# Folding and key stage: VectorE copies the turned context, and each group's high and low parts are made one slot later

## Chip, cores and metric

One core of a Trainium2 chip runs the whole program. The metric is its device time in microseconds; the median of three runs of the kernel before is 4688.49 us (4686.85 to 4693.32).

## What is computed

A decoder layer on 4 x 1024 tokens of width 512: windowed attention, cross attention with a context of 4 x 2048 x 384, state-space convolution and MLPs. The stage of this study prepares operands for later stages. Reduced to that:

```
K = x_vision @ Wk                       # keys: [8192, 384] @ [384, 128]
V = x_vision @ Wv                       # c_t = attn_mean @ V
film = c_t @ W_film_in, c_t @ W_film_out # so Wv @ W_film is made once (12 pieces)
h = einsum('bsd,dh->bsh', x, W_exp) + b_exp
h = butterfly(h, up_weights)            # 11 stages; the linear maps are folded into
h = gelu(h + up_bias)                   # W_exp (w3, b3) and W_con (w4) beforehand
h = butterfly(h, down_weights)
y = einsum('bsh,hd->bsd', h, W_con) + b_con
```

Keys are kept as a high part (the product rounded to fp32r) and a low part (the product less its high part).

## The kernel before

`decoder_layer` runs eight stages one after the other; each ends with all engines meeting. The second, `stage_butterfly_keys`, runs from about 270 to 569 us and merges three jobs on the same engines: folding the butterfly into the MLP weights, the film products, and the keys.

*Keys.* The context is cut in KG = 16 groups of 512 rows. For each group g SyncE loads `raw[g % 2]` (`context`, L603), TensorE turns its three 128-column parts in PE `keys_step` (L695, twelve transposes) into the two banks of `ps_t`, three copies (L840, on ScalarE) bring them to `cT` (which lies in the storage of `wx`, so the trace says `bf_wx`), and `project` (L681) multiplies them with `wk` into `ps_k`, which is the second bank of `ps_t`. TensorE runs `project(g - 1)` behind the turning of g. ScalarE writes the high part (`keys_hi`, L832), VectorE the low part (`keys_lo`, L939), SyncE stores both (`keys_stored`, L607). The second third of a turning waits until the low part of two groups before has been read out of the shared bank.

*Folding.* 4 top butterfly stages run over the down weights and later over the up weights (`group(1, i, g)`, i and g from 0 to 3). For each of 8 pairs ScalarE makes two scaled halves (`partners`, L812, L813), and VectorE makes a group of two pairs of them (L922, L927; four instructions). With i = 1 and 2 ScalarE also copies the turned down blocks (`down_copied`, L820) and the down products (`product_copied`, L826).

*Film.* Twelve products (`film`, L729), two banks; VectorE copies each (`film_copied`, L935) and SyncE stores it.

The order on each engine is written out by hand as interleaved loops; engines meet by semaphores only. TensorE: groups 0 and 1 with film 0 and 1; then groups 2 to 5 each with one film product; then the 16 down products (L766), with a key group behind every second one (groups 6 to 12) and film 6 and 7 in the middle; then groups 13 to 15 with film 8 to 10, the last `project`, film 11; last the row turning (L789), whose results are stored as w3. SyncE's queue has the stores of film 0 to 5 ahead of those of w4, and a load of context between w4's. ScalarE's `keys_step(g)` copies group g, then makes the high part of g - 1; VectorE's `keys_lo` follows behind a folding group and ahead of the film copy.

## Time and profile before

| | before |
|---|---|
| median of 3 runs, us | 4688.49 (4686.85 to 4693.32) |
| profiled execution, us | 4691.36, its span 4689.3 |
| mean granted TensorE clock | 0.927 |
| TensorE busy over the span | 3982.0 us (85%) |
| VectorE | 2527.2 us (54%) |
| ScalarE | 1470.2 us (31%) |
| GpSimd | 2009.3 us (43%) |

The profile is one execution. Its views used here: the stretches (busy time of each engine between two times), the waits (which instruction waited for which), the timeline of an engine (start, duration and idle time before each instruction, neighbours merged), and the groups of instructions by line. A granted clock of 1.0 is 2.4 GHz, 0.5 is 1.2 GHz.

### The profile page before, as it was taken

The page shows a single profiled execution, that of the slowest core. Times are in us where ns is not written, and L with a number is a line of the kernel's source. Part 1 is how long each engine was busy: PE and PEld are TensorE (multiplying, and loading weights), DVE is VectorE, ACT ScalarE, POOL GpSimd, SP SyncE. Part 2 cuts the span into 40 slices and gives each one's busy share as a digit, 9 for nine tenths or more (in the row PEclk, how much of TensorE's full clock was granted, in tenths as well). Part 3 has the DMA queues.
Part 4 walks back from the last instruction along what each step waited for, and adds up shares of the span by engine and source line. Part 5 has one row for each costly group of instructions (what it writes and reads, how often), then busy time and mean ns, then how long its engine had stood idle before and what let it go on. Part 6 is the DMA issues. An engine that isn't in the chain of part 4 may idle for free. (4 is left out here: it accounts for less than half of the span.)

```text
span 4689.3 us, 63710 instructions
## 1 busy us (share of the span) xinstructions
PE 3982.0 (85%) x20972; PEld 3269.0 (70%) x20972; DVE 2527.2 (54%) x8700; ACT 1470.2 (31%) x2339; POOL 2009.3 (43%) x1399
## 2 busy tenths in 40 slices
PE   6747599986866888888699697968999999999998
PEld 3633277765766778777688575757778877878886
DVE  8733355548888888888355555224344336222222
ACT  2344333325645666666200101212111112111111
POOL 0000011115756777777566042014677665333332
PEclk8659899997988999999799898988999999999999
DMA  1154522222010010100243333342222123000000
GB/s 59 37 167 153 169 77 90 83 70 59 15 45 28 25 52 15 49 28 12 83 147 134 109 118 134 115 131 88 64 70 77 60 76 97 25 21 25 22 25 18
DMA packets 248656, 336.41 MB, mean 72 GB/s; under 512 B 67587, under 2 KB 125859, under 8 KB 246053
## 3 DMA queue, kind: packets, MB, share of 16 engines
q1 hardware_dynamic: 156420, 186.18, 13.0%
q10 hardware_dynamic: 89392, 138.45, 8.7%
q0 software_dynamic: 2560, 8.39, 0.5%
q8 instruction: 130, 2.13, 0.2%
q14 instruction: 154, 1.25, 0.1%
HBM read 220.70 MB, written 112.25 MB: 71 GB/s over the span
## 5 line engine op out<-in xcount | busy, mean ns | idle before, releaser
L1647 PE MATMUL xa_ps_t<-xa_diag,xa_s_buf 128*128 128x128 f32 x4096 | 524.8, 289 | 139.7 <-ACT xa_a L1734 74.8
L2808 POOL TENSOR_TENSOR m_act_hl<-m_g,m_act_hl 128x512 fp32r<-128x512 f32 x256 | 355.6, 1389 | 660.0 <-DVE m_act_hl L3114 660.0
L1647 PEld LDWEIGHTS xa_ps_t<-xa_diag,xa_s_buf 128*128 128x128 f32 x4096 | 512.7, 204 | 160.5 <-issue 80.5
L3114 DVE CAST m_act_hl<-m_g 128x512 fp32r<-128x512 f32 x256 | 137.8, 538 | 832.2 <-ACT m_g L2982 832.2
L1811 DVE MAX8 xa_cand<-xa_s_buf 128x8 f32<-128x64 f32 x4096 | 543.0, 219 | 65.6 <-ACT xa_s_buf L1697 40.4
L2982 ACT ACTIVATE m_g<-m_ps_h,m_b 128x512 f32<-128x512 f32 x256 | 176.2, 688 | 1096.5 <-PE m_ps_h L82 1091.5
L80 PE MATMUL m_ps_h<-m_hT,m_w 128*128 128x512 f32 x1024 | 414.1, 404 | 6.3 <-issue 4.3
L80 PE MATMUL m_ps_o<-m_w,m_act_hl 128*128 128x512 f32 x1024 | 406.8, 397 | 0.7 <-POOL m_act_hl L2808 0.7
L82 PE MATMUL m_ps_h<-m_hT,m_w 128*128 128x512 f32 x1024 | 406.7, 397 | 0.0
L81 PE MATMUL m_ps_h<-m_hT,m_w 128*128 128x512 f32 x1024 | 406.7, 397 | 0.0
L82 PE MATMUL m_ps_o<-m_w,m_act_hl 128*128 128x512 f32 x1024 | 406.6, 397 | 0.0
L81 PE MATMUL m_ps_o<-m_w,m_act_hl 128*128 128x512 f32 x1024 | 406.4, 397 | 0.0
L1575 POOL TENSOR_SCALAR xa_s_buf<-xa_s_buf,xa_top 128x1024 f32<-128x1024 f32 x120 | 342.3, 2853 | 141.8 <-ACT xa_prob L1716 141.8
L1577 POOL TENSOR_TENSOR xa_s_buf<-xa_s_buf,xa_prob 128x1024 f32<-128x1024 f32 x120 | 321.1, 2676 | 18.2 <-issue 0.9
L1697 ACT ACTIVATE xa_s_buf<-xa_ps_s 128x2048 f32<-128x2048 f32 x128 | 239.6, 1872 | 145.3 <-PE xa_ps_t L1647 79.1
L1716 ACT ACTIVATE xa_prob<-xa_s_buf,xa_nmax 128x2048 f32<-128x2048 f32 x128 | 252.6, 1998 | 89.9 <-POOL xa_s_buf L1577 89.9
L1614 PE MATMUL xa_ps_s<-xa_ks,xa_qs 128*128 128x512 f32 x512 | 159.3, 435 | 126.8 <-ACT xa_s_buf L1697 111.7
L80 PEld LDWEIGHTS m_ps_h<-m_hT,m_w 128*128 128x128 f32 x1024 | 193.6, 189 | 56.1 <-issue 11.3
L80 PEld LDWEIGHTS m_ps_o<-m_w,m_act_hl 128*128 128x128 f32 x1024 | 193.2, 189 | 48.8 <-POOL m_act_hl L2808 1.9
L82 PEld LDWEIGHTS m_ps_h<-m_hT,m_w 128*128 128x128 f32 x1024 | 193.8, 189 | 47.1
L82 PEld LDWEIGHTS m_ps_o<-m_w,m_act_hl 128*128 128x128 f32 x1024 | 193.6, 189 | 47.0
L81 PEld LDWEIGHTS m_ps_o<-m_w,m_act_hl 128*128 128x128 f32 x1024 | 193.3, 189 | 47.0
(373 smaller groups left out, 8370.4 us busy)
## 6 DMA issues: line engine op xcount, KB each, us to landing
at_xk<-in_x_dram SPq DMA_DIRECT2D x128, 128.0 KB, 2.7
spectrum<-df_yo ACTq DMA_DIRECT2D x32, 512.0 KB, 2.8
id_raw<-spectrum SPq DMA_DIRECT2D x32, 512.0 KB, 5.7
m_xt<-x ACTq DMA_DIRECT2D x64, 256.0 KB, 3.8
bf_raw<-in_ctx_dram SPq DMA_DIRECT2D x16, 768.0 KB, 4.7
xa_ks<-kt SPq DMA_DIRECT2D x48, 256.0 KB
xa_raw<-in_ctx_dram SPq DMA_DIRECT2D x32, 384.0 KB, 3.4
kt<-bf_khl SPq DMA_DIRECT2D x16, 512.0 KB, 2.8
```

The source lines that it names most:

```text
L80: pe.matmul(out, w_hi, m_lo, start=start, stop=False)
L81: pe.matmul(out, w_lo, m_hi, start=False, stop=False)
L82: return pe.matmul(out, w_hi, m_hi, start=False, stop=stop)
L1575: pool.tensor_scalar(half, half, top[:, t % 2, h, TOPK - 1:TOPK], None, ALU.is_ge)
L1577: pool.tensor_tensor(half, half, prob[:, h % 2, HALF:S2], ALU.mult).then_inc(s_psel, 1)
L1614: last = pe.matmul(ps_s[:, c, :], qs[:, t % 2, h, :], ks[:, h, c * 512:(c + 1) * 512], start=True, stop=True)
L1647: last = pe.matmul(ps_t[:, c // 4, c % 4, :], s_buf[:, t % 2, h, k0:k0 + P], diag[:, h, :], start=(h == 0 and c % 4 == 0), stop=(h == HEAD ...
L1697: act.activation(s_buf[:, t % 2, h, :], ps_s[:, :, :].rearrange("p c n -> p (c n)"), ACT.Copy).then_inc(s_sc, 1)
L1716: act.activation(prob[:, h % 2, :], s_buf[:, t % 2, h, :], ACT.Exp, bias=nmax[:, t % 2, h:h + 1], scale=SCALE).then_inc(s_exp, 1)
L1811: dve.max(out=ranks[h][:, :, g], in_=s_buf[:, t % 2, h, :].rearrange("p (n g e) -> p g n e", g=SEGS, e=4)[:, g, :, :])
L2808: pool.tensor_tensor(lo, g32[:, :], hi.bitcast(F32), ALU.subtract).then_inc(s_gl, 1)
L2982: act.activation(g32[:, :], ps_h[:, n % 2, :], ACT.Gelu, bias=b1[:, cur, n:n + 1]).then_inc(s_g, 1)
```

## The change

VectorE gets a `keys_step(g)`: low part of g - 2, a wait for the key product of g - 2, then the three copies of the turned group g into `cT`. ScalarE loses its `keys_step` with the 48 copies and keeps `keys_hi`, called for one group earlier at each place (a slot later for a given group). On SyncE the store of a key group is also a step later (g - 2 instead of g - 1), and the last one stands behind all film stores. TensorE's order and all waits of TensorE are the same.

```diff
--- before.py
+++ after.py
@@ -610,8 +610,8 @@
                 def keys_step(g):
                     if g + 2 < KG:
                         context(g + 2)
-                    if g >= 1:
-                        keys_stored(g - 1)
+                    if g >= 2:
+                        keys_stored(g - 2)
 
                 sp.wait_ge(s_wx[1], 16)
                 sp.dma_start(wv[:, :, :], A["L0_xattn_Wv"].rearrange("(c p) n -> p c n", p=P)).then_inc(s_wv, 16)
@@ -645,9 +645,10 @@
                 for n in range(FILM, FILM + 3):
                     keys_step(KG - 3 + n - FILM)
                     film_stored(n)
-                keys_stored(KG - 1)
+                keys_stored(KG - 2)
                 for n in range(FILM + 3, 2 * FILM):
                     film_stored(n)
+                keys_stored(KG - 1)
                 for n in range(4 * DC):
                     sp.wait_ge(s_rc[n % 2], n // 2 + 1)
                     c, g = n // 4, n % 4
@@ -831,16 +832,6 @@
                         act.wait_ge(s_kst[g % 2], 16 * (g // 2))
                     act.activation(khl[:, g % 2, 0, :], ps_k[:, :], ACT.Copy).then_inc(s_khi, 1)
 
-                def keys_step(g):
-                    if g >= 2:
-                        act.wait_ge(s_k, g - 1)
-                    for c in range(VC):
-                        n = VC * g + c
-                        act.wait_ge(s_t, n + 1)
-                        act.activation(cT[:, g % 2, c, :], ps_t[:, c % 2, :], ACT.Copy).then_inc(s_tc, 1)
-                    if g >= 1:
-                        keys_hi(g - 1)
-
                 act.wait_ge(s_cdn, 16 * 4)
                 for q in range(HC // 2):
                     if q % 2 == 0:
@@ -866,13 +857,11 @@
                         h = (HC // 2) * (i - 2) + q
                         act.wait_ge(s_mm, h + 1)
                         act.activation(wT[:, h, 0:D], ps[:, h % 2, :], ACT.Copy).then_inc(s_mmc, 1)
-                keys_step(0)
-                keys_step(1)
                 for i in range(TOP):
                     for q in range(HC // 2):
                         partners(1, i, q)
                         if i == 0 and q % 2 == 1:
-                            keys_step(2 + q // 2)
+                            keys_hi(q // 2)
                         if i == 1:
                             if q == 0:
                                 down_copied(0)
@@ -883,9 +872,10 @@
                             if h + 2 < HC:
                                 down_copied(h + 2)
                             if h % 2 == 1 and h < HC - 1:
-                                keys_step(FILM + h // 2)
+                                keys_hi(FILM - 2 + h // 2)
                         if i == TOP - 1 and q in (1, 3, 5):
-                            keys_step(KG - 3 + q // 2)
+                            keys_hi(KG - 5 + q // 2)
+                keys_hi(KG - 2)
                 keys_hi(KG - 1)
                 for n in range(0, 16, 2):
                     act.wait_ge(s_r, n + 1)
@@ -937,6 +927,14 @@
                 def keys_lo(g):
                     dve.wait_ge(s_khi, g + 1)
                     dve.tensor_tensor(khl[:, g % 2, 1, :], ps_k[:, :], khl[:, g % 2, 0, :].bitcast(F32), ALU.subtract).then_inc(s_klo, 1)
+
+                def keys_step(g):
+                    if g >= 2:
+                        keys_lo(g - 2)
+                        dve.wait_ge(s_k, g - 1)
+                    for c in range(VC):
+                        dve.wait_ge(s_t, VC * g + c + 1)
+                        dve.tensor_copy(cT[:, g % 2, c, :], ps_t[:, c % 2, :]).then_inc(s_tc, 1)
 
                 dve.wait_ge(s_cdn, 16 * 4)
                 for g in range(GROUPS):
@@ -962,16 +960,17 @@
                 dve.drain().then_inc(s_bias, 1)
                 dve.wait_ge(s_ms, 16)
                 dve.tensor_scalar(mask[:, :], mask_u8[:, :], BIG, -BIG, ALU.mult, ALU.add).then_inc(s_mask, 1)
-                keys_lo(0)
+                keys_step(0)
+                keys_step(1)
                 for i in range(TOP):
                     for g in range(GROUPS):
                         group(1, i, g)
                         if i < 2:
-                            keys_lo(GROUPS * i + g + 1)
-                        elif i == 3:
-                            keys_lo(KG - GROUPS + g)
+                            keys_step(GROUPS * i + g + 2)
                         elif g < GROUPS - 1:
-                            keys_lo(2 * GROUPS + g + 1)
+                            keys_step(GROUPS * i + g + 2 - (i - 2))
+                        elif i == TOP - 1:
+                            keys_lo(KG - 2)
                         if i == 0:
                             film_copied(g)
                         if i == 1 and GROUPS + g < FILM:
@@ -980,6 +979,7 @@
                             film_copied(FILM + g)
                 for n in range(FILM + GROUPS, 2 * FILM):
                     film_copied(n)
+                keys_lo(KG - 1)
                 dve.tensor_tensor(upb[:, :], upb[:, :], wT[:, :, D], ALU.add)
                 dve.drain().then_inc(s_hi, 1)
                 for n in range(1, 16, 2):
```

## Rows read from the trace of the kernel before

**Rows 1.** stretches: busy us of each engine (instructions), TensorE's granted clock, DMA share, GB/s

```profile
357.00:538.00 181.00, 135.35 (x431) 67.09 (x430) 73.81 (x111) 88.44 (x165) 0.00 (x0) 0.94 0.45 157
```

**Rows 2.** waits from 357 to 538 us: us in total, times, longest

```profile
PE bf_ps_w L729 <- DVE bf_fo L935: 16.6, 8, 2.1
```

**Rows 3.** timeline of TensorE, one film slot: start us, us, line, idle before and releaser

```profile
402.61 1.04 PE L695 MATMUL bf_ps_t<-bf_ident,bf_raw 128*128 128x128 f32 x8
...
404.45 2.84 PE L681 MATMUL bf_ps_t<-bf_wx,bf_wk 128*128 128x512 f32 x6
409.36 3.70 PE L729 MATMUL bf_ps_w<-bf_low_up,bf_wvT 128*128 128x512 f32 x8 [2.07 <-DVE bf_fo L935]
412.89 1.04 PE L695 MATMUL bf_ps_t<-bf_ident,bf_raw 128*128 128x128 f32 x8
```

**Rows 4.** timelines of ScalarE and VectorE, the same slot

```profile
403.31 1.08 ACT L840 ACTIVATE bf_wx<-bf_ps_t 128x512 f32<-128x512 f32 x2 [3.23 <-PE bf_ps_t L695]
...
407.32 0.60 ACT L832 ACTIVATE bf_khl<-bf_ps_t 128x512 fp32r<-128x512 f32 x1 [2.08 <-PE bf_ps_t L681]
...
407.95 0.69 DVE L939 TENSOR_TENSOR bf_khl<-bf_ps_t,bf_khl 128x512 fp32r<-128x512 f32 x1 [4.92 <-ACT bf_khl L832]
408.56 0.74 DVE L935 TENSOR_SCALAR bf_fo<-bf_ps_w,bf_gate 128x512 f32<-128x512 f32 x1
410.40 1.42 DVE L922 SCALAR_TENSOR_TENSOR bf_wT<-bf_wT,bf_col_up,bf_part 128x513 f32<-128x513 f32 x2 [1.10 <-ACT bf_part L813]
411.90 1.42 DVE L927 SCALAR_TENSOR_TENSOR bf_wT<-bf_wT,bf_col_up,bf_part 128x513 f32<-128x513 f32 x2
```

**Rows 5.** groups of instructions by line, 200 to 1100 us: busy us, mean ns, idle before

```profile
L840 ACT ACTIVATE bf_wx<-bf_ps_t 128x512 f32<-128x512 f32 x48 | 27.3, 603 | 36.2 <-PE bf_ps_t L695 36.2
...
L988 DVE COPY bf_out_t<-bf_ps 128x512 f32<-128x512 f32 x8 | 5.5, 692 | 16.3 <-DMA w<-bf_out_t 13.8 <-PE bf_ps L789 2.5
```

**Rows 6.** timelines of VectorE and TensorE at the start of the keys

```profile
368.72 0.67 DVE L939 TENSOR_TENSOR bf_khl<-bf_ps_t,bf_khl 128x512 fp32r<-128x512 f32 x1
...
378.18 2.98 PE L695 MATMUL bf_ps_t<-bf_ident,bf_raw 128*128 128x128 f32 x12 [5.28 <-DMA bf_raw<-in_ctx_dram]
380.95 4.12 PE L681 MATMUL bf_ps_t<-bf_wx,bf_wk 128*128 128x512 f32 x6
```

**Rows 7.** timeline of TensorE in the down product and the tail

```profile
428.65 2.84 PE L681 MATMUL bf_ps_t<-bf_wx,bf_wk 128*128 128x512 f32 x6
431.33 0.27 PE L756 MATMUL bf_ps_e<-bf_ident,bf_e_dn 128*128 128x128 f32 x1
...
451.82 2.82 PE L681 MATMUL bf_ps_t<-bf_wx,bf_wk 128*128 128x512 f32 x6
...
465.13 2.84 PE L681 MATMUL bf_ps_t<-bf_wx,bf_wk 128*128 128x512 f32 x6
...
489.89 2.84 PE L681 MATMUL bf_ps_t<-bf_wx,bf_wk 128*128 128x512 f32 x6
...
500.66 3.97 PE L681 MATMUL bf_ps_t<-bf_wx,bf_wk 128*128 128x512 f32 x6
...
539.16 1.04 PE L789 MATMUL bf_ps<-bf_ident,bf_wT 128*128 128x128 f32 x8
```

**Rows 8.** timelines of ScalarE and VectorE in the down product

```profile
444.75 0.60 ACT L826 ACTIVATE bf_out_t<-bf_ps 128x512 f32<-128x512 f32 x1 [3.15 <-DMA w<-bf_out_t]
...
478.45 0.28 ACT L820 ACTIVATE bf_eT<-bf_ps_e 128x128 f32<-128x128 f32 x1
478.61 0.73 ACT L812 ACTIVATE bf_part<-bf_wT,bf_col_up 128x513 f32<-128x513 f32 x1
...
479.98 1.42 DVE L922 SCALAR_TENSOR_TENSOR bf_wT<-bf_wT,bf_col_up,bf_part 128x513 f32<-128x513 f32 x2 [2.40 <-ACT bf_part L813]
```

**Rows 9.** timeline of TensorE in a later stage: a wait of 2.97 us

```profile
1456.99 6.33 PE L1647 MATMUL xa_ps_t<-xa_diag,xa_s_buf 128*128 128x128 f32 x32 [2.97 <-ACT xa_a L1734]
```

**Rows 10.** stretch right behind that wait, columns as in the first group

```profile
1457.00:1461.00 4.00, 4.00 (x19) 4.00 (x20) 3.71 (x26) 0.74 (x2) 4.00 (x3) 0.50 0.42 129
```

## The prediction

> **What bounds the kernel now.** The page's span is the whole program; the edit touches one stage only, which runs from about 270 to 569 us, and in it the stretch from 357 us, where the first context group is turned, to 539 us, where the row turning (L789) begins. So I read, in this order: the busy times of that stretch, its waits, then the timelines of TensorE, ScalarE and VectorE side by side, slot by slot. Over 181 us TensorE is busy 135 us, ScalarE 88 and VectorE 74 [rows 1]: no engine is full, so waits between engines set the pace, and TensorE, in whose order everything hangs, is nearest to the bound. Its costliest wait on VectorE is the film product for the film copy (L729 on L935), 16.6 us in 8 waits [rows 2]; the timeline of a film slot shows where it comes from. The turning starts at 402.61, the key product (L681) at 404.45, the film product only at 409.36, the next turning at 412.89 [rows 3]: a slot of 10.28 us. The key product needs 2.68 us (428.65 to 431.33, [rows 7]), so 4.91 - 2.68 = 2.2 us of each slot are a wait: VectorE's film copy (408.56) stands behind the low part (407.95), which stands behind ScalarE's high part (407.32), which waits for this slot's key product [rows 4].
>
> In the second part (down product, 423 to 500 us) a steady slot takes (489.89 - 465.13)/3 = 8.25 us between key products [rows 7]. There ScalarE is the chain: high part, partners, product copy, block copy, partners, product copy, block copy, three context copies. All other stages only move with the end of this one, so the sum is made here.
>
> **Part 1: film slots, T(3) to the end of film(5).** (T(g) is the turning of context group g, P(g) the start of its key product; P(g-1) runs in the slot of T(g).) The high part a slot later takes the 2.2 us wait away: the film copy no longer stands behind this slot's key product. What it costs: a VectorE copy from PSUM takes 692 ns against ScalarE's 603 [rows 5], and neighbours start 0.61 apart (407.95, 408.56) against 0.48 (the pair at 403.31 takes 1.08) [rows 4]. From turning to key product it was 1.84 us [rows 3]; with the first copy's start 0.70 after the turning, + 0.61 + 0.69 + 0.05, it becomes 2.05. New slot: 2.05 + 2.68 + 3.53 (film, 409.36 to 412.89) = 8.26 us. Is VectorE fast enough? From its first copy x: third copy x + 1.43, film copy x + 2.04, folding group x + 2.7 for 3.0 us (two halves 1.50 apart, [rows 4]), low part x + 5.7 to 6.4. The bank is wanted at about x + 7.6 + 0.4: it is in time by 1.6 us. ScalarE has only 2.5 us of partners and 0.6 of high part per slot. Three slots give 3 x 2.02 = **-6.0 us**.
>
> **Part 2: the start.** ScalarE copied groups 0 and 1 at 359 to 364 us, while VectorE made the down blocks; VectorE now comes to them only where low part 0 began, 368.72 [rows 6]. TensorE stands with the last third of T(0) from 358.3 to 369.4 and then runs at the lower clock. Copies 0.69, T(0)'s last third 1.1, copy, T(1) 2.0, copy: P(0) at about 374.1, 4.1 us at the low clock (the row at 380.95 has 4.12, against 2.84 [rows 6, 7]), film(0) and film(1) 7 us: T(2) at 385 instead of 378.18. The old T(2) waited for a load and paid the low clock itself: 378.18 to T(3) at 392.3, 14.1 us. The new one, warm, takes 8.3: T(3) at 393.3, **+1.0 us** (-1.3 with a warm first product, +3 with one film product at the low clock). The load of group 2 isn't late: it is issued at 370.7 and had 10 us before.
>
> **Part 3: entry to the down product.** Here ScalarE's order bites. Its partners for the second of a group's two pairs stand behind a block copy (down_copied), which needs a block turned on TensorE *after* the key product; VectorE now does that folding group before the low part and the copies, and so before the next key product can start. Before, ScalarE copied the context while VectorE folded beside it. First slot, on the old clock of rows: group from 427.0 (unchanged) to 430.0, low part 0.6, copies: P(5) at 432.1 instead of 428.65 [rows 7]: **+3.5 us**.
>
> **Part 4: the steady loop.** From P: key product 2.68, block turned 0.27 + 0.04 (the row at 431.33), block copy, partners 0.16 later, group 1.53 after the block copy (478.45 to 479.98) [rows 8], so the group starts at P + 4.5; folding 3.0; low part at P + 7.5; then 0.61 + 0.72 (turning into the freed bank) + 0.1 + 0.69 to the next P: P + 9.63. As a check the old chain added in the same way gives 8.26 and the rows 8.25. Three steady slots P(8) to P(11): 3 x 1.38 = **+4.1 us**. P(11) to P(12) took 10.77 (489.89 to 500.66 [rows 7]) since two pairs and product copies lie between; the new chain (product copy of block 15 at P + 3.7, four partners to 6.8, group to 9.8, 2.1) is 12.2 with a cold start: **+1.4 us**.
>
> **Part 5: P(5) to P(8),** before 428.65 to 465.13, 36.5 us, with a stall that stays: SyncE keeps the first stores of w4 and the load of group 8 behind film_stored(5), so ScalarE waits to 444.75 [rows 8]. The film copy 5 comes at about 442.3 (old clock; before 441.0), ScalarE then starts at 446.0, group to 451, P(7) at 453.4 against 451.82 [rows 7]; then two film products, as before, and P(8) at 467.1. 432.1 to 467.1 is 35.0: **-1.5 us**. The store of key part g now is issued one step later; the high part of g + 2 needs it, and has more than 4 us over in every slot, at the stall about none.
>
> **Part 6: the tail, P(12) to the row turning,** before 500.66 to 539.16, 38.5 us, with four waits for the film copy. New: key product at the low clock 3.9, film 3.5, turning 2.05 (P(13) at 9.5), slot 8.3, then 6.2 and 6.2: 30.2. **-8.3 us**. **Part 7: the end.** The last low part (0.6) now comes behind the last film copy and its 512 KB store into the stores of w3, which fill the DMA engines: **+1.0 us** (0.6 to 1.6).
>
> Sum: -6.0 + 1.0 + 3.5 + 4.1 + 1.4 - 1.5 - 8.3 + 1.0 = -4.8 us.
>
> **The clock.** The new loop leaves TensorE idle about 3.1 us in one piece per slot (from the first third of the turning at P + 5.1 to P + 8.25), before at most 1.5. The trace has no such gap in this stage; the nearest: 2.2 us gaps left 1.0 in nearly all film slots (one beside the low clock of 387), while a gap of 2.97 us at 1456.99 is followed by 0.50 [rows 9, 10], which is the 1.2 GHz level. A key product at it costs 4.12 - 2.84 = 1.3 us. Bounds: none of the loop's slots, 0, to all six (P(5), P(6), P(9) to P(12)) at 1.9 with the turning, 11. I take three slots at 1.2, **+3.5**, nearer the row of 2.97 than that of 2.2 but mostly with part of the product. The Trainium skill (TensorE: Matmul & The Clock Gate, "HAM oscillation") says that a loop with such a wait pays the transition in every iteration; by it the sum would be near the upper bound. The rows here bear it out for 2.97 us and not for 2.2.
>
> Net -1.3 us on the profiled execution's own 4691.36 (span 4689.3 and 2.1 around it), which lies 2.9 above the median of the three runs shown; on the median 4688.49: **4687.2 us**. About 0.2% (9.4 us) is what a measurement of this kernel can tell from no change.
>
> **The rivals.** *Gaps throttle TensorE (slower):* all six gaps bring the low clock (+11), and at the start a film product too (+2): -4.8 + 13 = +8, with the end at its upper bound and another cold slot at the stall +10: 4698 us. It turns slower once the clock falls in more than three loop slots. For: the row at 1456.99 [rows 9, 10]; against: the key product is only partly in the slow time where it falls. 0.20 in all, of it 0.11 over 0.2%. *The loop does not close (faster):* if ScalarE's partners were ready early, a slot of the down product would be 7.2 us (key product, two down products, high and low part, copy): Part 3 falls to 0, Part 4 to -3.2 and -1: -4.8 - 3.5 - 7.3 - 2.4 = -18, 4670 us. For: ScalarE loses 29 us of copies; against: the written order puts down_copied ahead of the second partners, and nothing in the change moves it. 0.07. *The film gains stay and the clock holds (mildly faster):* -4.8 to -11 us, 4679, when the start costs nothing either: 0.20, of it 0.07 beyond 0.2%. *Nothing arrives at the end,* as the final stores of w3 and the wait for them fill what was gained: 4688, 0.10. The forecast, gains and losses cancelling within some 5 us: 0.43.
>
> **The numbers.** Leaving out half of the two far cases, the range runs from 4677 to 4698. Faster by over 0.2%: 0.07 + 0.07 = 0.14; slower by over 0.2%: 0.11; within: 0.75.
>
> **What would show it.** T(2) at about 385 us; no wait of L729 on the film copy; film slots 8.3 us and the film stretch over near 418 instead of 423; from there slots of about 9.6 us with the folding group, low part and three copies in a row on VectorE, and ScalarE's second partners waiting on a block turned after the key product; the row turning near 534 to 538 instead of 539.2. Wrong if the slots there are nearer 7 (the loop does not close) or 11 (clock), if VectorE's low part is late in the film slots, or if a load of context shows up ahead of a turning.

## The result, and the profile after

| | before | after |
|---|---|---|
| time, median of 11 runs each, us | 4688.49 (4682.72 to 4694.88) | 4698.27 (4694.53 to 4706.42) |
| ratio after / before, 95% interval | | 1.0021 (1.0013 to 1.0029) |
| profiled execution, us (span) | 4691.36 (4689.3) | 4704.4 (4702.4) |
| first context turning T(0) / row turning / first instruction of the attention stage, us | 357.25 / 539.16 / 569.9 | 356.42 / 543.40 / 576.9 |

The change costs 9.8 us, 0.21%. The forecast was 4687.2 us, -1.3, with a range that ended at 4698: the time lies just above its end, and the sign is that of the rival "gaps throttle TensorE". The two profiled executions differ by 13 us, and 7 of these have arisen when the attention stage begins. All medians in this document leave out two executions that took far longer than the rest, one of before (6561.55 us) and one of e9_bias_hidden (8547.19 us).

First the same stretch as [rows 1] in the profile after (busy us of TensorE, its weight loads, VectorE, ScalarE, GpSimd, each with its instructions, then TensorE's granted clock, DMA share, GB/s), with a window over the steady loop:

```profile
357.00:538.00 181.00, 138.43 (x417) 70.68 (x415) 103.05 (x157) 60.53 (x114) 0.00 (x0) 0.86 0.46 151
...
465.00:490.00 25.00, 18.37 (x61) 9.78 (x60) 13.40 (x20) 10.31 (x21) 0.00 (x0) 0.84 0.46 147
```

As the edit says, 28 to 29 us of work have gone from ScalarE to VectorE. TensorE has done less of its work in the stretch (417 instructions for 431) in more busy time: the granted clock fell from 0.94 to 0.86. The waits of the same stretch (us in total, times, longest):

```profile
DVE bf_wT L912 <- ACT bf_part L814: 42.2, 8, 8.5
...
PE bf_ps_t L696 <- DVE bf_khl L929: 25.1, 8, 6.5
...
PE bf_ps_t L696 <- DVE bf_wx L937: 14.5, 8, 11.1
...
ACT bf_out_t L827 <- DMA w<-bf_out_t: 7.4, 1, 7.4
...
ACT bf_khl L833 <- DMA kt<-bf_khl: 3.6, 1, 3.6
```

The wait of the film product for the film copy [rows 2] is in the whole list no more. In its place TensorE waits at the turning (L696) for VectorE's low part (L929), which stands behind the folding group (L912), which waits for ScalarE's partners. The 11.1 us is the start; the last line was not in the forecast.

TensorE in a film slot of after (start us, us, line, idle before and releaser), the slot that answers to [rows 3]:

```profile
400.50 1.04 PE L696 MATMUL bf_ps_t<-bf_ident,bf_raw 128*128 128x128 f32 x8
401.95 0.66 PE L696 MATMUL bf_ps_t<-bf_ident,bf_raw 128*128 128x128 f32 x4 [0.42 <-DVE bf_wx L937]
402.55 2.84 PE L682 MATMUL bf_ps_t<-bf_wx,bf_wk 128*128 128x512 f32 x6
405.23 3.60 PE L730 MATMUL bf_ps_w<-bf_low_up,bf_wvT 128*128 128x512 f32 x8
408.66 0.60 PE L696 MATMUL bf_ps_t<-bf_ident,bf_raw 128*128 128x128 f32 x4
```

The film product follows the key product at once, and the slot takes 8.16 us instead of 10.28. Now TensorE in the down product, where [rows 7] had 8.25 us from key product to key product (L682):

```profile
467.13 2.84 PE L682 MATMUL bf_ps_t<-bf_wx,bf_wk 128*128 128x512 f32 x6 [0.19 <-DVE bf_wx L937]
469.92 1.02 PE L767 MATMUL bf_ps<-bf_wc,bf_eT 128*128 128x512 f32 x2
470.89 1.02 PE L767 MATMUL bf_ps<-bf_wc,bf_eT 128*128 128x512 f32 x2
471.75 0.60 PE L696 MATMUL bf_ps_t<-bf_ident,bf_raw 128*128 128x128 f32 x4
475.43 1.97 PE L696 MATMUL bf_ps_t<-bf_ident,bf_raw 128*128 128x128 f32 x8 [3.08 <-DVE bf_khl L929]
477.33 5.04 PE L682 MATMUL bf_ps_t<-bf_wx,bf_wk 128*128 128x512 f32 x6
482.32 1.02 PE L767 MATMUL bf_ps<-bf_wc,bf_eT 128*128 128x512 f32 x2
483.29 1.02 PE L767 MATMUL bf_ps<-bf_wc,bf_eT 128*128 128x512 f32 x2
484.15 0.60 PE L696 MATMUL bf_ps_t<-bf_ident,bf_raw 128*128 128x128 f32 x4
487.83 1.57 PE L696 MATMUL bf_ps_t<-bf_ident,bf_raw 128*128 128x128 f32 x8 [3.08 <-DVE bf_khl L929]
489.28 4.20 PE L682 MATMUL bf_ps_t<-bf_wx,bf_wk 128*128 128x512 f32 x6
```

Each slot has the wait of 3.08 us that the forecast worked out (3.1), and behind it a key product of 5.04 or 4.20 us where 2.84 is the time at full clock; two turned thirds take 1.97 and 1.57 instead of 1.25. The slots are 10.2 and 12.0 us. VectorE in the same slot is the loop in one view:

```profile
471.65 1.42 DVE L912 SCALAR_TENSOR_TENSOR bf_wT<-bf_wT,bf_col_up,bf_part 128x513 f32<-128x513 f32 x2 [3.98 <-ACT bf_part L814]
473.15 1.42 DVE L917 SCALAR_TENSOR_TENSOR bf_wT<-bf_wT,bf_col_up,bf_part 128x513 f32<-128x513 f32 x2
474.69 0.69 DVE L929 TENSOR_TENSOR bf_khl<-bf_ps_t,bf_khl 128x512 fp32r<-128x512 f32 x1
475.29 0.68 DVE L937 COPY bf_wx<-bf_ps_t 128x512 f32<-128x512 f32 x1
476.59 0.69 DVE L937 COPY bf_wx<-bf_ps_t 128x512 f32<-128x512 f32 x1 [0.61 <-PE bf_ps_t L696]
477.44 0.69 DVE L937 COPY bf_wx<-bf_ps_t 128x512 f32<-128x512 f32 x1 [0.16 <-PE bf_ps_t L696]
```

The key product of 467.13 is over at 469.92, then block, partners, a folding group of 3.0 us, low part, copies, next key product. The group is the longest link, and nothing in the low part or the copies needs it: it only stands ahead in VectorE's order. And ScalarE waits in its turn for the block turned behind the slow key product:

```profile
482.52 0.28 ACT L821 ACTIVATE bf_eT<-bf_ps_e 128x128 f32<-128x128 f32 x1 [8.06 <-PE bf_ps_e L757]
```

### The profile page after: what moved, and what is told of

It reads as the page before. It is cut to its first block and busy times, and to the rows that moved or that the text cites. A ratio compares the mean times of both kernels' runs of the same rounds, so it can differ in the third digit from the quotient of the medians.

```text
span 4702.4 us, 63710 instructions
## 1 busy us (share of the span) xinstructions
PE 3992.6 (85%) x20972; PEld 3276.8 (70%) x20972; DVE 2560.9 (54%) x8748; ACT 1443.6 (31%) x2291; POOL 2008.4 (43%) x1399
## 5 line engine op out<-in xcount | busy, mean ns | idle before, releaser
L1564 POOL TENSOR_TENSOR xa_aT<-xa_a,xa_aT 128x512 fp32r<-128x512 f32 x128 | 161.9, 1284 | 153.5 <-ACT xa_a L1734 153.5
L80 PEld LDWEIGHTS m_ps_o<-m_w,m_act_hl 128*128 128x128 f32 x1024 | 193.2, 189 | 48.8 <-POOL m_act_hl L2808 2.0
L82 PEld LDWEIGHTS m_ps_o<-m_w,m_act_hl 128*128 128x128 f32 x1024 | 193.6, 189 | 47.0
```

The costliest lines, as they stand in the source:

```text
L80: pe.matmul(out, w_hi, m_lo, start=start, stop=False)
L82: return pe.matmul(out, w_hi, m_hi, start=False, stop=stop)
L1564: pool.tensor_tensor(aT[:, 1, 4 * g:4 * g + 4, :], a32[:, g % 2, :, :], aT[:, 0, 4 * g:4 * g + 4, :].bitcast(F32), ALU.subtract).then_inc( ...
```

## The experiments

Counted from T(0), the traces give these times (us; P(g) is the start of group g's key product, as in the forecast; the last column is how long the attention stage takes). The time of a run is compared with runs of the kernel before on the same chip. Two of the kernels are before and after once more.

```
kernel             P(5)   P(8)-P(11)  P(12)  row turning  stage ends at  attention
before             71.4   24.8        143.4  181.9        569.9          489.9
before again       69.6   24.8        142.3  184.6        571.3          488.2
after              69.9   33.7        157.6  187.0        576.9          493.2
after again        70.2   31.9        157.0  187.0        574.4          492.2
e1_steps_first     66.7   23.5        141.8  171.4        560.3          490.2
e2_fill_gap        68.8   29.2        150.0  178.5        568.0          493.0
e3_scalar_start    63.8   32.8        151.1  180.8        568.6          494.2
e4_delay_alone     63.3   31.8        147.7  178.5        568.6          487.3
e5_copies_alone    79.4   36.4        171.5  214.8        601.9          491.1
e6_reordered       61.6   23.5        123.4  153.5        543.5          493.8
e7_bias_early      69.8   32.7        156.8  186.5        577.1          493.6
e8_before_padded   68.7   24.7        141.0  183.1        569.5          494.0
e9_bias_hidden     62.6   23.5        124.8  155.2        542.3          491.9
e10_padded_back    61.5   23.6        125.4  156.1        542.0          487.1
```

My theory after the result: the loop through the folding group (longer than before by 1.4 us a slot) and the low clock behind its waits cost what the film slots gain; rivals were the clock alone, the start, and the moved copies as such.

**The order on VectorE** (e1_steps_first). Edit on the kernel after: in the second film turn and the down product the folding group comes behind the low part and the copies.

```diff
                     for g in range(GROUPS):
-                        group(1, i, g)
+                        if i not in (1, 2):
+                            group(1, i, g)
...
                             keys_lo(KG - 2)
+                        if i in (1, 2):
+                            group(1, i, g)
```

> The changed kernel, but in the down product (i = 1 and 2) VectorE does the low part and the three context copies ahead of the folding group instead of behind it. Theory (order: the group, fed by ScalarE partners that wait for a block turned after the key product, stands in series with the next key product): P(8) to P(11) falls from 33.7 us to about 23 (7.7 a slot), TensorE's waits on the low part fall from 3.1 us to under 1, its clock stays at 1.0, P(5) starts 3 us after the last down product; the row turning starts 15 to 20 us earlier and the time is 4675 to 4682 us. Rival (VectorE's copies are simply dearer and slower than ScalarE's): the same copies at the same price, so the slots stay above the old 8.25 us and the time stays within 3 us of 4698.

Measured: 4684.08 us (4679.72 to 4691.04), before 4686.41; ratio 0.9995 (0.9986 to 1.0004). TensorE in the steady loop of this kernel:

```profile
469.61 2.84 PE L682 MATMUL bf_ps_t<-bf_wx,bf_wk 128*128 128x512 f32 x6 [0.19 <-DVE bf_wx L937]
...
476.02 1.25 PE L696 MATMUL bf_ps_t<-bf_ident,bf_raw 128*128 128x128 f32 x8 [1.19 <-DVE bf_khl L929]
477.45 2.84 PE L682 MATMUL bf_ps_t<-bf_wx,bf_wk 128*128 128x512 f32 x6 [0.18 <-DVE bf_wx L937]
```

The slot is 7.85 us, the wait 1.19, every key product of the loop is at full clock, and the row turning comes 15.6 us earlier than in after. So the folding group in VectorE's order is the loop's cause. The time itself, 14.2 us below after, ends up only level with before: 2 us above the expectation, where the stage ends 9.6 us earlier than before's. The attention stage, behind it, gives back none of this; what is lost there was found below.

**The clock by itself** (e2_fill_gap). Edit: the same waits stay, but TensorE turns identity tiles into the bank that isn't in use while it waits.

```diff
                             pe.wait_ge(s_tc, VC * g)
+                        if c == 0 and 6 <= g <= 13:
+                            for _ in range(16 if g < 13 else 40):
+                                pe.transpose(ps_t[:, 0, 0:P], ident[:, :], ident[:, :])
                         if c == 1 and g >= 2:
```

> The changed kernel with added work only: ahead of the first third of each turning of groups 6 to 12 TensorE turns the identity 16 times more, 40 times for group 13, into a bank that the real turning overwrites, so that its wait for the low part is partly filled (16 cost 1.8 us at the full clock). Theory, part two (the waits let the clock fall to 1.2 GHz): key products P(5) to P(12) return from 3.4-4.9 us to 2.7, which is 9.7 us in all, P(8) to P(11) falls from 33.7 to about 29 us, the time to about 4689. Rival (the order alone costs it, the clock matters little): the slots keep their 11.2 us and the time is 4698 or more.

Measured: 4693.13 us (4683.41 to 4695.66); ratio 1.0010 (1.0001 to 1.0019). In the window from 465 to 500 us TensorE's granted clock, 0.84 in after's loop, is here 1.00 (columns as above):

```profile
465.00:500.00 35.00, 30.45 (x157) 19.38 (x156) 18.96 (x28) 17.28 (x35) 0.00 (x0) 1.00 0.65 208
```

All key products of P(5) to P(12) take 2.81 to 2.84 us, P(8) to P(11) takes 29.2 us, three slots of 9.73, and the row turning comes 8.5 us earlier than in after. The time is 5.1 us below after, some 4 above the 4689 expected. The 16 identity turns also cost something where TensorE hardly had to wait: before the turning ahead of P(8) the wait was 0.28 us in after, and here VectorE's copies wait 1.62 us for TensorE at that place. So 8.5 us is less than the clock took. This splits the loop: 29.2 against before's 24.8 is the chain (+4.4; the forecast had +4.1), 33.7 against 29.2 is the clock (+4.5 for three slots, where the forecast had +3.5 for all).

**The start** (e3_scalar_start). Edit: ScalarE copies groups 0 and 1 again, VectorE's first two steps are gone.

```diff
+                for n in range(2 * VC):
+                    g, c = n // VC, n % VC
+                    act.wait_ge(s_t, n + 1)
+                    act.activation(cT[:, g % 2, c, :], ps_t[:, c % 2, :], ACT.Copy).then_inc(s_tc, 1)
                 for i in range(TOP):
                     for q in range(HC // 2):
...
-                keys_step(0)
-                keys_step(1)
```

> The changed kernel, but ScalarE copies groups 0 and 1 as before, VectorE the other fourteen. Theory: the start costs the change 1 us in net, since the old one waited for a load; T(2) comes at about 378 after the load instead of 384, at the low clock, and all of it shifts by 2 to 4 us: 4694 to 4697. Rival (the 11 us of idle TensorE at the start is the loss): T(2) 6 us earlier and the time 4692 or less.

Measured: 4690.10 us (4683.41 to 4698.64); ratio 1.0004 (0.9994 to 1.0013). The row turning comes 6.2 us earlier than in after, more than the 2 to 4 expected, and the time lies where the rival had it (4692 or less): T(2), in this kernel's TensorE timeline, waits for its load as in before [rows 6]

```profile
360.82 2.84 PE L682 MATMUL bf_ps_t<-bf_wx,bf_wk 128*128 128x512 f32 x6
363.50 7.03 PE L730 MATMUL bf_ps_w<-bf_low_up,bf_wvT 128*128 128x512 f32 x16
375.66 3.08 PE L696 MATMUL bf_ps_t<-bf_ident,bf_raw 128*128 128x128 f32 x12 [5.13 <-DMA bf_raw<-in_ctx_dram]
```

Counted from T(0), T(2) comes at 20.8 us (375.66 less 354.87), as in before (20.9), where after had 27.8 (384.17 less 356.42), and the film product behind it doesn't wait. So the start costs 6 us against what the late high part could have, though only 0.8 against before (T(3) at 392.33 less 356.42, before 392.3 less 357.25), whose own film product there had the wait for the film copy.

**The delay alone, on the kernel before** (e4_delay_alone). ScalarE keeps the copies, but makes a group's high part one slot later, VectorE the low part, SyncE the store.

```diff
                     if g >= 2:
                         act.wait_ge(s_k, g - 1)
+                        keys_hi(g - 2)
                     for c in range(VC):
...
-                    if g >= 1:
-                        keys_hi(g - 1)
...
                         if i < 2:
-                            keys_lo(GROUPS * i + g + 1)
+                            keys_lo(GROUPS * i + g)
                         elif i == 3:
-                            keys_lo(KG - GROUPS + g)
+                            keys_lo(KG - GROUPS + g - 1)
```

> The kernel before with the delay alone: high and low part of group g - 2 in the slot of group g, but ScalarE keeps all 48 copies. Theory (the low part behind the folding group is what ties the loop, not who copies): film slots lose their 2.2 us wait (8.1 us a slot), the slots of the down product go to 9.5 us and more with waits for the low part of about 3 us and the low clock, time within 5 us of the changed kernel, 4693 to 4700. Rival (moving the copies to VectorE makes the loop): the down slots stay at 8.25 and the film gain of some 14 us shows: 4676.

Measured: 4686.41 us (4679.57 to 4689.47); ratio 0.9996 (0.9987 to 1.0005). TensorE in its loop:

```profile
477.96 1.97 PE L696 MATMUL bf_ps_t<-bf_ident,bf_raw 128*128 128x128 f32 x8 [3.08 <-DVE bf_khl L940]
479.76 3.55 PE L682 MATMUL bf_ps_t<-bf_wx,bf_wk 128*128 128x512 f32 x6
```

The same wait of 3.08 us and the same low clock, with the copies still on ScalarE: P(8) to P(11) takes 31.8 us. The bad loop comes with the delay, since the low part sits behind this slot's folding group; the film slots are 8.2 us, so the gain comes with the delay too. But the time is that of before, not the 4693 to 4700 expected: the stage ends 8.3 us earlier than in after, of which the start is some 6, and the attention stage takes 487.3 us instead of 493.2, for a reason found below.

**The copies alone, no delay** (e5_copies_alone). On the kernel after, high part, low part and store go back to their old slot (ten lines; the core of them):

```diff
-                        keys_lo(g - 2)
                         dve.wait_ge(s_k, g - 1)
                     for c in range(VC):
                         dve.wait_ge(s_t, VC * g + c + 1)
                         dve.tensor_copy(cT[:, g % 2, c, :], ps_t[:, c % 2, :]).then_inc(s_tc, 1)
+                    if g >= 1:
+                        keys_lo(g - 1)
```

> The changed kernel without the delay: VectorE copies the context, but high and low part of group g - 1 stay in the slot of group g, as before the change. Theory (each of the two parts alone ties the down product's loop, since either the low part or the copies stand behind the folding group; the film gain is the delay's; the late start is the copies'): film slots 10.5 us with their wait for the film copy, T(2) at 384, P(8) to P(11) 28 to 33 us, the slowest kernel of all, 4702 to 4712 us. Rival (the two parts only do harm together): the down slots stay near 8.3 us and the time is 4690 to 4696.

Measured: 4723.02 us (4721.71 to 4724.16); ratio 1.0079 (1.0066 to 1.0093), slower than the 4702 to 4712 expected. Its waits from 357 to 570 us:

```profile
DVE bf_khl L928 <- ACT bf_khl L832: 51.3, 16, 4.7
...
PE bf_ps_w L729 <- DVE bf_fo L924: 16.6, 8, 2.1
```

Film slots are 10.5 to 12.2 us, the film product waits as before, and now VectorE itself stands 51.3 us at the low part, with the folding groups behind it. So the two halves of the change belong together: the copies on VectorE cost 30 to 33 us at the row turning without the delay, and with it 8.5 (after against the delay alone), of which 6 are the start.

**Putting the order right** (e6_reordered). On the kernel after: the two edits above (ScalarE's start, the group behind the step), the same order for the first group of the last turn with the high part of group 11 right behind the last product copy, the stores of film 4 and 5 moved on SyncE from ahead of the stores of w4 to between them, and the store of the 8 KB bias issued behind the first output copy (the edit of e7_bias_early below).

```diff
-                for n in range(FILM):
-                    if n < GROUPS:
-                        keys_step(2 + n)
+                for n in range(GROUPS):
+                    keys_step(2 + n)
                     film_stored(n)
...
+                    if n in (1, 3):
+                        film_stored(GROUPS + n // 2)
...
-                        group(1, i, g)
+                        late = i in (1, 2) or (i == TOP - 1 and g == 0)
+                        if not late:
+                            group(1, i, g)
...
+                        if i == TOP - 1 and g == 0:
+                            film_copied(FILM)
+                        if late:
+                            group(1, i, g)
...
-                            if h % 2 == 1 and h < HC - 1:
+                            if h % 2 == 1:
                                 keys_hi(FILM - 2 + h // 2)
```

> A version that may beat both, from the changed kernel: ScalarE copies groups 0 and 1; VectorE's low part and copies ahead of the folding group in the down product and for group 13, whose high part of group 11 comes right behind the last product copy; SyncE stores film 4 and 5 between the stores of w4 instead of ahead of them; the bias b3 is stored behind ScalarE's first row copy instead of its last. Theory: T(3) 5 us earlier, no wait of ScalarE for a store of w4 (4 us and the low clock behind it), no 6.4 us wait at group 13, no bias store at the end (some 5 us): the stage 18 to 28 us shorter than in the kernel before and 4660 to 4672 us. Rival (the stores of the stage fill the DMA engines, so that what is gained ahead is waited for at the end): no better than 4680.

Measured: 4666.52 us (4665.29 to 4670.39), before 4685.84; ratio 0.9961 (0.9947 to 0.9975), faster by 0.39%. The stage ends 26.4 us earlier than in before, but the time is only 19.3 lower. Again some us are lost behind the stage. Against e1_steps_first the row turning comes 17.9 us earlier: 5.1 of it are there at P(5) (the start), 9.5 arise from P(5) to P(8) (29.6 us for 39.1) and 3.8 from P(11) to P(12). In e1 ScalarE waited 8.2 us for a store of w4 and 3.4 us for the store of key part 4 between P(5) and P(8); here it waits for neither. So the largest part is put down to the two film stores, by the timelines: no kernel moved them alone.

**The end of the stage** (e7_bias_early). Edit on the kernel after: the bias store is issued after the first of the output copies, not after the last.

```diff
                     act.activation(out_t[:, n % 4, :], ps[:, n % 2, :], ACT.Copy).then_inc(s_rc[0], 1)
-                act.wait_ge(s_hi, 1)
-                act.dma_start(b3_out.rearrange("(c p) -> p c", p=P), upb[:, :], allow_slow_non_contiguous=True).then_inc(s_b3, 16)
+                    if n == 0:
+                        act.wait_ge(s_hi, 1)
+                        act.dma_start(b3_out.rearrange("(c p) -> p c", p=P), upb[:, :], allow_slow_non_contiguous=True).then_inc(s_b3, 16)
```

> The changed kernel with the bias store b3 issued behind ScalarE's first row copy instead of its last, nothing else. Theory (from the row turning's start the stage took 30.8 us before and 33.5 after; the last to land is this store, 12.8 us behind ScalarE's last copy): the turning to the next stage's start falls by 4 to 8 us and the time to 4691 to 4695. Rival (the last stores of w3 land as late, so the bias store is beside them): 33 us stay and the time stays at 4698.

Measured: 4701.45 us (4700.39 to 4703.63); ratio 1.0035 (1.0021 to 1.0049): no gain, the rival was right. The window behind the row turning in this kernel, where the bias store is in it:

```profile
545.00:560.00 15.00, 2.67 (x16) 1.99 (x16) 1.05 (x2) 1.19 (x2) 0.00 (x0) 0.66 1.08 114
```

and in after, where only the 256 KB stores are in it, then the window of the bias store there, with its size (KB) and its time to landing (us):

```profile
545.00:560.00 15.00, 9.40 (x56) 6.73 (x53) 5.58 (x9) 4.18 (x7) 0.00 (x0) 0.89 0.88 297
...
557.00:577.00 20.00, 0.98 (x7) 0.50 (x5) 1.37 (x2) 0.60 (x1) 0.07 (x1) 0.58 0.69 62
...
b<-bf_upb ACTq DMA_DIRECT2D x1, 8.0 KB, 12.8
```

By the edit's access pattern the 8 KB go out as 4-byte elements; in after they take 12.8 us to land. Placed among the 256 KB stores they leave the DMA engines as busy (share 1.08 for 0.88) but moving 114 GB/s instead of 297, and a row copy of ScalarE waits 12.8 us for a store of w3.

**Both kernels once more** (a2_after_again, b2_before_again), to see what belongs to the kernel and what to one execution.

> The changed kernel itself, once more: a second profile and its time on this chip. Theory: the same slots (P(8) to P(11) 32 to 35 us, since where the low clock begins shifts between executions), stage length within 3 us of the first, ratio 1.0015 to 1.003; the 6 us by which the stages behind this one were longer in the first profile (4125.5 against 4119.4 us) are of that execution alone, so here 4116 to 4128. Rival (VectorE's longer instruction stream costs something in the stages behind): again 4125 or more.

Measured: 4697.30 us (4693.0 to 4700.8); ratio 1.0025 (1.0014 to 1.0035). The row turning is at the same place to 0.1 us. The stages behind took 4121.3 us: within the 4116 to 4128 of the expectation, and not the 4125 of the rival; over all kernels (below) a part of the rival holds.

> The kernel before itself, once more, for a second profile: no VectorE wait of over 1 us without releaser in the attention stage, key products P(8) to P(11) 24.8 us apart at the full clock, turning start about 181.9 us behind T(0), the stages behind the folding stage within 3 us of 4119.

Measured: 4683.4 us in one execution. Row turning at 184.6 after T(0) instead of 181.9, stage end at 571.3, and the stages behind took 4110.1 us, not within 3 of 4119. So one execution of before can be 2.7 us later there, and the change's price at the row turning is 2.4 to 5.1 us.

**What is lost behind the stage.** Nothing that the change touches lies in the attention stage, yet it took 489.9 us in before and 493.2 in after. VectorE's and TensorE's timelines of after near 835 us show the place:

```profile
834.84 1.13 DVE L1339 TENSOR_SCALAR at_tT<-at_ps_t,at_u_k 128x128 f32<-128x128 f32 x4 [1.69 <-issue]
836.21 0.69 DVE L1328 SCALAR_TENSOR_TENSOR at_dot<-at_xq,at_u_q 128x512 f32<-128x512 f32 x1 [0.24 <-issue]
837.68 0.08 DVE L1328 DVE_READ_ACCUMULATOR at_dot<-at_xq,at_u_q 128x1 f32 x1 [0.78 <-issue]
```

```profile
836.05 3.10 PE L1184 MATMUL at_ps_s<-at_xT,at_tT 128*128 128x256 f32 x8 [2.12 <-DVEq L1340]
```

and the DMA queues of the window from 832 to 839 us have packets of instructions:

```profile
q14 instruction: 3, 0.02, 1.0%
```

VectorE's wait of 1.69 us has no releaser in the profile, and it is the only one of its kind over 1 us in the stage. The packets do not say which engine they feed, and alone they prove nothing: before has 16 packets of this queue in the stage and no such wait. TensorE waits 2.12 us for it, and its next product takes 3.10 us where the same 8 take 1.99 in the last kernel below. VectorE's trace has 11629 instructions in before and 11691 in after: 48 copies came in, and with their waits it is 62. My theory: the boundary between two pieces of VectorE's instruction stream has moved from somewhere harmless into the busy part of a block, with no link to what the change computes. The Trainium skill (Advanced Engine Details and Errata, "ISA Cache") has an engine's instruction cache in lines of 256 instructions; that section names no price.

Test (e8_before_padded): the kernel before with 62 one-column memsets on VectorE at the end of the stage, where it is idle, and nothing else.

```diff
+                for k in range(62):
+                    dve.memset(pad[:, k:k + 1], 0.0)
         st.clear()
```

> The kernel before with 62 small memsets added to VectorE behind its last row copy, where it is idle until the stage ends; the changed kernel's VectorE stream is 62 instructions longer too. Theory (in all kernels with the longer stream VectorE once waits for instructions in the attention stage, some 260 us into it, 1.7 and 0.8 us without any releaser, with three packets of an instruction queue beside it and the lower TensorE clock behind it, which costs 3 to 4 us; it belongs to where the stream is cut, not to the new order): the same stall at the same tile, folding stage as before, time 3 to 5 us above the kernel before. Rival (it comes from the new order or from ScalarE's shorter stream): no stall, time within 1 us of it.

Measured: 4692.44 us (4687.46 to 4699.53), before 4687.6; ratio 1.0012 (1.0003 to 1.0021). The same stall at the same tile, in VectorE's timeline:

```profile
828.23 1.13 DVE L1342 TENSOR_SCALAR at_tT<-at_ps_t,at_u_k 128x128 f32<-128x128 f32 x4 [1.66 <-issue]
...
831.39 0.08 DVE L1331 DVE_READ_ACCUMULATOR at_dot<-at_xq,at_u_q 128x1 f32 x1 [1.11 <-issue]
```

The attention stage takes 494.0 us. Instructions that do nothing, at an idle place, cost the kernel before 0.12%. So the wait belongs to the length of VectorE's instruction stream, whatever the added instructions do.

**The two remedies.** First on the reordered kernel (e9_bias_hidden): the bias is added right behind the last folding group instead of behind the last film copies, and its store goes out ahead of the last high part.

```diff
                 keys_hi(KG - 2)
+                act.wait_ge(s_hi, 1)
+                act.dma_start(b3_out.rearrange("(c p) -> p c", p=P), upb[:, :], allow_slow_non_contiguous=True).then_inc(s_b3, 16)
                 keys_hi(KG - 1)
...
                         elif i == TOP - 1:
+                            dve.tensor_tensor(upb[:, :], upb[:, :], wT[:, :, D], ALU.add)
+                            dve.drain().then_inc(s_hi, 1)
                             keys_lo(KG - 2)
```

> The reordered version (e6) with the bias computed right behind the last folding group and stored behind ScalarE's high part 14, ahead of the tail's film copies, instead of behind the first row copy. Theory (the bias store holds the DMA engines for 11 to 14 us wherever it stands, so it helps only where nothing else wants them): the row turning to the next stage's start falls from 33.7 us to about 26, the time to 4658 to 4662. Rival (then the stores of film 9 to 11 and of the last key parts wait for it and film copy 11 with them): the turning starts 4 to 6 us later and the time stays at 4666.

Measured: 4664.06 us (4661.61 to 4668.13), before 4687.6; ratio 0.9951 (0.9937 to 0.9964); 4658 to 4662 were expected. From the row turning to the stage's end it takes 30.2 us, for 33.7 in e6_reordered (543.5 - 356.3 - 153.5); 26 were expected. But the row turning itself comes 1.7 us later (155.2 for 153.5), so the stage ends only some 1.8 us earlier. Second, on that (e10_padded_back), 200 memsets on VectorE, so that its stream is 256 instructions longer than in before (56 from the copies, 200 of padding; pieces of 256, if there are such, would begin where they began):

```diff
+                for k in range(110):
+                    dve.memset(pad[:, k:k + 1], 0.0)
                 dve.wait_ge(s_cdn, 16 * 4)
...
+                for k in range(110, 200):
+                    dve.memset(pad[:, k:k + 1], 0.0)
```

> The version with the bias moved (e9), whose VectorE stream is 56 instructions longer than before's up to the attention stage, padded with 200 small memsets in VectorE's idle times of the folding stage, so that all behind lies 256 instructions later than in the kernel before. Theory (VectorE's stream is loaded in pieces of a fixed number of instructions, 256 or a divisor of it, and the stall belongs to a boundary): no 1.7 us wait without releaser in the attention stage, which takes 488 to 490 us instead of 491.9, and 4660 to 4663 us. Rival (what counts is the total length or the shorter ScalarE stream, or the pieces have another size): the stall stays or moves, time 4665 or more.

Measured: 4656.12 us (4651.18 to 4659.95), before 4689.41; ratio 0.9925 (0.9912 to 0.9939), the fastest kernel here, 0.75% below before. The wait at L1339's tile is gone, the attention stage takes 487.1 us, and TensorE's product has its old length (timeline):

```profile
838.52 1.99 PE L1198 MATMUL at_ps_s<-at_xT,at_tT 128*128 128x256 f32 x8 [0.40 <-DVEq L1354]
```

All ten profiled kernels with 56 or 62 instructions more had a wait of 1.7 to 2.2 us at that tile; the three without shift (before twice, and the delay alone) and the one shifted by 256 had none. The attention stage took 490.2 to 494.2 us with it (median 493.1) and 487.1 to 489.9 without (487.8): some 5 us by the medians, though the nearest two values are 0.3 apart (490.2 and 489.9). A shift of 256 without the wait fits the 256 instructions of the Trainium skill's "ISA Cache" (Advanced Engine Details and Errata); it does not show them, since no other shift than 56, 62 and 256 was tried.

Everything behind the folding stage (the span less the stage's end) took 4119.6 to 4128.0 us in the ten (median 4122.4) and 4110.1 to 4119.4 in the four (4115.4): 7 us, of which the attention stage explains some 5. What the rest is was not looked for.

## Why the prediction was wrong

The working, by its own parts:

- **Part 1, film slots.** Right. Slot 8.16 us (forecast 8.26); the wait of L729 is gone; block turnings begin at 416.82 instead of 423.18, 6.4 us earlier, 0.8 of it from an earlier T(0); -5.0 was forecast with the start in it. VectorE was in time, as worked out.
- **Part 2, the start.** Right: T(3) came 0.8 us later after T(0), +1.0 forecast. That a possible gain of 6 us lay in it was not seen.
- **Part 3, entry.** Right: P(5) at 426.32. On the rows' time scale the forecast was 432.1; less the 5.0 of Parts 1 and 2 and the 0.8 of the earlier T(0) that is 426.3.
- **Part 4, the loop.** The chain was right (9.73 us a slot with the clock held, forecast 9.63; the wait 3.08 for 3.1). P(8) to P(11) measured 33.7 for a forecast of 28.9 ahead of the clock.
- **Part 5.** One term was missing. ScalarE's high part of group 6 waited 3.6 us for the store of key part 4; "about none" was wrong at the stall, since the delay puts that store a step later in SyncE's order, behind the stall. About 1.9 of it is on TensorE's path, by the timelines; no kernel tried it alone. P(5) to P(8) took 40.8 us where 35.0 were forecast, but some 5.0 of the 5.8 between are the clock's.
- **Part 6, the tail.** Right: P(12) to the row turning took 29.4 us, 9.1 less than before (8.3 forecast).
- **The clock.** Here the step failed. The term took 3 slots at 1.2 us = 3.5. Measured: TensorE waited 2.6 to 6.5 us ahead of seven of the eight key products from P(5) to P(12), and all seven ran 0.7 to 2.2 us over 2.84, together 9.7 us; the turnings between wait and key product took another 2.3. That is about 12 us, 1.7 a slot, of which P(12) had about 1.1 in the kernel before too (3.97 for 2.84, [rows 7]): 11 us net, the forecast's upper bound. The sum without the clock put the row turning 5.8 us earlier than before, and it came 5.1 later: the 10.9 between are about the clock's 11. Filling the waits gave back 8.5 of them. The rule of the Trainium skill named in the forecast (TensorE: Matmul & The Clock Gate, "HAM oscillation"), that the price is paid in every iteration, agrees with these traces in seven of eight slots.
- **Part 7, the end.** Row turning to the attention stage took 33.5 us for 30.8: +2.8, forecast +1.0, upper bound 1.6. In the second executions it was 31.9 for 30.8, +1.1, so this term is not shown to be wrong.
- **Outside the sum.** The forecast held that "All other stages only move with the end of this one". They don't: the attention stage lost 3.3 us (493.2 for 489.9; 492.2 and 488.2 in the second executions) to the longer instruction stream of VectorE.

**The row that the clock term was taken from** was misread. The forecast has the wait of 2.97 us at 1456.99 "followed by 0.50" [rows 9, 10]. The stretches ahead of it in the trace of before show that the clock was at 0.50 already:

```profile
1447.00:1451.00 4.00, 0.42 (x4) 0.22 (x3) 3.55 (x2) 1.99 (x3) 4.00 (x3) 1.00 0.52 153
1451.00:1454.00 3.00, 2.92 (x16) 2.64 (x16) 2.55 (x20) 0.00 (x0) 3.00 (x2) 0.67 0.26 70
1454.00:1457.00 3.00, 0.03 (x2) 0.04 (x1) 2.77 (x18) 2.95 (x6) 2.25 (x3) 0.50 0.73 238
```

It fell behind the wait before that one, of 3.66 us. TensorE's timeline of before has that wait, and one of 4.96 us in this stage ahead of P(12), whose key product took 3.97 us [rows 7]:

```profile
1451.08 2.94 PE L1647 MATMUL xa_ps_t<-xa_diag,xa_s_buf 128*128 128x128 f32 x16 [3.66 <-DVE xa_s_buf L1866]
```

```profile
499.75 1.12 PE L695 MATMUL bf_ps_t<-bf_ident,bf_raw 128*128 128x128 f32 x4 [4.96 <-ACT bf_wx L840]
```

So no row of the forecast showed what a wait of 3 us does: waits of 2.07 us mostly left the full clock, those of 3.66 and 4.96 did not. With nothing in between, three slots was a guess between 0 and 11 and should have been called one. That a wait of 3.08 us in every slot brings the low clock is what the run after was the first to show.

So the 9.8 us are made up of the folding stage, about +3 to +7 at its end (574.4 and 576.9, against 569.9 and 571.3), and the longer instruction stream, some 5 (padding alone measured 0.12%, 5.6 us, interval 0.03 to 0.21%). The rival "gaps throttle TensorE" had the right mechanism at 0.20; its time, 4698, was reached with a cause beside it that no case named, so that it fits to 0.3 us is luck. What stays open: executions of one kernel differ by several us (the stages behind the folding stage took 4119.4 and 4110.1 us in the two of before), so the two parts can't be told to the last us. And e10_padded_back lies 33.3 us below before on its chip, e9_bias_hidden 23.5 on its own: of the 9.8 between them the stall explains about half.

## What to carry to other kernels

When a late step (here the low part) frees the bank that the matrix engine wants, put it ahead of independent work in its engine's order: with the 3 us folding group behind it the same change was level with before instead of 0.21% slower, and with the start left on ScalarE, the last turn ordered likewise and two film stores out of the way of the stores of w4 0.39% faster. Price a wait of the matrix engine that recurs in every slot with the clock for every slot. Before a row is used for what a wait does to the clock, read the granted clock ahead of that wait too; and where the rows leave a hole, as here between 2.07 and 3.66 us, give both ends of it a case instead of a value in the middle. And when a change adds or takes away instructions, look in all later stages for idle time that waits for "issue" beside packets of the instruction queue; compare with a padded kernel before reasoning about a difference of 0.1%.

## What the runs showed of the hardware

- With 56 or 62 more instructions in VectorE's stream, even memsets at an idle place, VectorE waited once in the attention stage for 1.7 to 2.2 us without a releaser (ten kernels), in five of them for another 0.7 to 1.1 at a later instruction, and the stage took about 5 us more; in after TensorE stood 2.12 us behind it and ran its next product in 3.10 instead of 1.99. With none or with 256 more the wait was not there (four kernels).
- Waits of 3.08 us in slots of 10 to 12 us left key products of 3.4 to 5.0 us behind them (granted clock 0.84 over the loop, 1.00 with the wait filled); waits of 1.19 us left 2.84. The one key product of the loop with a wait of only 0.28 us ahead (P(8), 467.13) had full clock.
- An 8 KB store in 4-byte elements took 12.8 us to land. Among the output stores it left the DMA engines at a share of 1.08 with 114 GB/s, for 0.88 with 297 GB/s without it, so moving it there gained nothing; ahead of the last high part it shortened the stage's end by 3.5 us and delayed the row turning by 1.7.
- On VectorE a low part and the copy behind it, both of 128x512 from PSUM, start 0.60 us apart (474.69, 475.29) at 0.69 each: the second starts before the first is over.
